# Ten patch chunks in f16 parts in place of eight, the normalised input written by ScalarE, its transposition behind four f16 chunks

## What is computed

```python
patches = X.reshape(B, C, 8, 28, 8, 28).transpose(0, 2, 4, 1, 3, 5).reshape(B, 64, 2352)
tokens = einsum('bpi,hi->bph', patches, W) + b          # 2352 -> 128
h = concatenate([cls, tokens], axis=1) * pos_embed      # 65 tokens of 128
h = h + lstm(layernorm(h))                              # 65 steps over the tokens
h = h + moe(layernorm(h))                               # 16 experts, the best 2, 128 -> 512 -> 128, exact gelu
```

## Time and profile before

| | before |
|---|---|
| median of three executions | 693.02 |
| the profiled execution's own time | 692.99 |
| its span (first to last instruction) | 691.2 |
| PE busy | 622.2 (90%) |
| PE's weight loads busy | 589.8 (85%) |
| VectorE busy | 569.0 (82%) |
| ScalarE busy | 489.4 (71%) |
| GpSimd busy | 414.4 (60%) |
| mean granted clock of PE | 0.96 |

### The profile page before, as it was taken

How to read it: one execution, slowest core, us unless ns; L and a number is a source line. 1 busy time by engine, 2 the same in 40 slices (tenths; PEclk the granted TensorE clock), 3 DMA queues, 4 the chain that set the end, 5 groups by cost and what they waited for, 6 DMA issues and landing times.

```text
span 691.2 us, 24716 instructions
## 1 busy us (share of the span) xinstructions
PE 622.2 (90%) x7952; PEld 589.8 (85%) x7952; DVE 569.0 (82%) x1839; ACT 489.4 (71%) x1335; POOL 414.4 (60%) x446
## 2 busy tenths in 40 slices
PE   4899999999999999999999779999999999999400
PEld 4899999999999999999989668799888899889300
DVE  3787888888888888888898868988888888888487
ACT  3587777666666667665555467788888888888465
POOL 0133333587776776677577666777777666666500
PEclk9999999999999999999999889999999999999855
DMA  8987787787888888878862233455543343332198
GB/s 315 371 276 271 266 282 248 251 267 268 269 272 264 270 270 261 268 244 259 251 218 91 74 90 92 126 160 168 147 122 108 105 108 105 110 113 74 32 374 340
DMA packets 72472, 141.68 MB, mean 205 GB/s; under 512 B 13142, under 2 KB 55714, under 8 KB 64414
## 3 DMA queue, kind: packets, MB, share of 16 engines
q1 hardware_dynamic: 62704, 121.69, 55.1%
q0 software_dynamic: 9280, 17.21, 7.1%
q10 hardware_dynamic: 366, 1.21, 0.5%
HBM read 116.35 MB, written 25.66 MB: 205 GB/s over the span
## 4 chain that ended last, share of the span: by engine, by line
PE 63%; DVE 7%; DMA 4%; issue 3%; POOL 2%; ACT 2%; POOLq 0%; SPq 0%; ACTq 0%; DVEq 0%
PE bank L1137 22%; PE bank L1292 14%; PE bank L1310 14%; PE bank L1183 4%; DMA patches<-back 3%; PE bank L1147 3%; PE bank L1266 2%; PE bank L1152 1%; PE bank L1238 1%; POOL sent L1093 1%; DVE patches L987 1%; ACT patches L646 1%; PE bank L1209 1%; PE bank L1162 1%; PE bank L1172 1%
## 5 line engine op out<-in xcount | busy, mean ns | idle before, releaser
L1115 POOL DMA_INDIRECT back<-patches x160 | 156.5, 978 | 64.9 <-issue 53.2
L1137 PE MATMUL bank<-ws,patches 128*128 128x128 f32 (+1 forms) x1408 | 173.2, 279 | 9.1 <-DMA patches<-in_x 9.1
L1093 POOL DMA_INDIRECT sent<-pay,slot_own x130 | 151.6, 1166 | 39.4 <-issue 36.1
L1137 PEld LDWEIGHTS bank<-ws,patches 128*128 128x128 f32 (+1 forms) x1408 | 164.1, 194 | 9.2 <-issue 7.5
L609 ACT ACTIVATE bank<-bank,b1s 128x256 f32<-128x256 f32 x320 | 130.7, 453 | 37.1 <-PE bank L1292 36.7
L553 ACT ACTIVATE gate<-bank,lbias 128x128 f32<-128x128 f32 x260 | 74.1, 367 | 82.2 <-PE bank L1152 82.2
L987 DVE TENSOR_TENSOR patches<-bank,patches 128x512 f16<-128x512 f32 x160 | 109.4, 684 | 26.3 <-ACT patches L618 21.6
L1310 PE MATMUL bank<-ex_hi,patches 128*128 x1280 | 112.5, 220 | 3.6 <-DVE patches L1003 2.9
L1292 PE MATMUL bank<-patches,ex_hi 128*128 128x256 f16 x640 | 111.2, 276 | 2.5 <-DVE patches L987 1.5
L1105 POOL TENSOR_TENSOR rstd<-veps,cst 128x2 f32<-128x2 f32 (+1 forms) x68 | 57.4, 844 | 87.8 <-DVE veps L734 86.4
L618 ACT ACTIVATE patches<-bank 128x512 f16<-128x512 f32 x160 | 97.6, 611 | 0.0
(11 more groups left out here) (139 smaller groups left out, 1406.6 us busy)
## 6 DMA issues: line engine op xcount, KB each, us to landing
patches<-in_x SPq DMA_DIRECT2D x62, 1152.0 KB
patches<-sent SPq DMA_DIRECT2D x80, 130.0 KB
patches<-back SPq DMA_DIRECT2D x13, 640.0 KB, 6.5
ex_raw<-in_we SPq DMA_DIRECT2D x64, 128.0 KB
patches<-in_b SPq DMA_DIRECT2D x80, 64.0 KB
posr<-in_pos SPq DMA_DIRECT2D x65, 64.0 KB
out_tower<-h SPq DMA_DIRECT2D x13, 320.0 KB, 5.3
back<-patches POOLq DMA_INDIRECT x160
```

The costliest lines, as they stand in the source:

```text
L1093: pool.indirect_dma_start(sent, bass.IndirectOffsetOnAxis(ap=slot_own[:, g % 4, choice, col:col + 1], axis=0), pay[:, t % NP, :], None, bo ...
L1115: pool.indirect_dma_start(back, bass.IndirectOffsetOnAxis(ap=dsti[j % NO][:, k:k + 1], axis=0), yo[j % NO][:, k, :], None, bounds_check=2 ...
L1137: last = pe.matmul(bank_of, l, w_, start=(c == KS and k == 0), stop=(c == KS - 1 and k == 2))
```

## The change

The number of f16 chunks KS goes from 8 to 10 (so nine f32 products of a patch, the rest's among them, in place of eleven), the number of raw expert buffers NE from 7 to 5. `xn` is written by ScalarE, between the tanh and the second half of the split, as `h0 * rstd + shift2`; so `shift2` gets a second column for the input, written by one VectorE instruction for both rows, and a second buffer per column. VectorE's `xn` instruction goes. On PE `transpose_x` stands behind four f16 chunks of the projection instead of ahead of all of them. The lines that load the gelu table after the last tanh stand now under a condition on t0 = n + 2 that is false for n = T - 1 = 64, so they are never issued. The diff:

```diff
--- before.py
+++ after.py
@@ -30,7 +30,8 @@
 KC = IN_D // P
 KREST = IN_D - KC * P
 KBIAS = 64
-KS = 8
+KS = 10
+KMID = 4
 E, FF = 16, 512
 FC = FF // P
 TOKENS = T * B
@@ -47,7 +48,7 @@
 PIECE = 256
 PIECES = E * 2 * FF // PIECE
 TWICE = 16
-NE = 7
+NE = 5
 UG = 8
 SIZES = [8] * 6 + [6, 4, 4, 3]
 EARLY_GROUPS = 6
@@ -131,7 +132,7 @@
         mv = sb("mv", [P, 2, 2])
         veps = sb("veps", [P, 2])
         rstd = sb("rstd", [P, 2])
-        shift2 = sb("shift2", [P, 2])
+        shift2 = sb("shift2", [P, 2, 2])
         xn = sb("xn", [P, 2, HID])
         xT_hi = sb("xT_hi", [HID, 2, B], F16)
         xT_lo = sb("xT_lo", [HID, 2, B], F16)
@@ -572,6 +573,13 @@
                 if 0 <= n <= T - 1:
                     through(act, c_done, n)
                     act.activation(tc[:, :], c2, ACT.Tanh, scale=0.5).then_inc(tc_done, 1)
+                t0 = n + 2
+                if 0 <= t0 <= T - 1:
+                    act.wait_ge(shift_done, normed(n))
+                    if t0 >= 2:
+                        through(act, xT_ps, t0 - 2)
+                    act.activation(xn[:, t0 % 2, :], h0[:, t0 % 4, :], ACT.Identity, bias=shift2[:, n % 2, 0:1],
+                                   scale=rstd[:, 0:1]).then_inc(xn_done, 1)
                     if n == T - 1:
                         act.activation(warm[:, :], cst[:, C_ONE:C_ONE + 1], ACT.Gelu)
                 if halved:
@@ -581,10 +589,10 @@
                 t = token_at(shifts, n)
                 if t >= 0:
 
-                    through(act, shift_done, t)
+                    act.wait_ge(shift_done, normed(t + 1))
                     if t >= NP:
                         rows_sent(act, t - NP)
-                    act.activation(pay[:, t % NP, 0:HID], h1[:, t, :], ACT.Identity, bias=shift2[:, t % 2:t % 2 + 1],
+                    act.activation(pay[:, t % NP, 0:HID], h1[:, t, :], ACT.Identity, bias=shift2[:, (t + 1) % 2, 1:2],
                                    scale=rstd[:, 1:2]).then_inc(yn_done, 1)
                 t = n + 2
                 if 0 <= t <= T - 1:
@@ -740,20 +748,16 @@
                     through(dve, cab_done, n)
                     dve.scalar_tensor_tensor(c2, cab[:, 0, :], 0.5, cab[:, 1, :], ALU.mult, ALU.add).then_inc(c_done, 1)
                     routing(n)
-                def shift_of(t):
-
-                    dve.wait_ge(rstd_done, normed(t + 1))
-                    dve.scalar_tensor_tensor(shift2[:, t % 2:t % 2 + 1], mv[:, 1, 0:1], -1.0, rstd[:, 1:2], ALU.mult,
+                def shift_of(n, both):
+
+                    dve.wait_ge(rstd_done, normed(n))
+                    if n >= 1 and both.start == 0:
+                        through(dve, xn_done, n)
+                    dve.scalar_tensor_tensor(shift2[:, n % 2, both], mv[:, both, 0], -1.0, rstd[:, both], ALU.mult,
                                              ALU.mult).then_inc(shift_done, 1)
 
-                if pre and post:
-                    shift_of(t1)
                 if pre:
-                    dve.wait_ge(rstd_done, normed(n))
-                    if t0 >= 2:
-                        through(dve, xT_ps, t0 - 2)
-                    dve.tensor_scalar(xn[:, t0 % 2, :], src0, mv[:, 0, 0:1], rstd[:, 0:1], ALU.subtract,
-                                      ALU.mult).then_inc(xn_done, 1)
+                    shift_of(n, both)
                 if 0 <= n <= T - 1:
 
                     through(dve, tc_done, n)
@@ -767,7 +771,7 @@
                                       ALU.subtract).then_inc(h_lo_done, 1)
                 t = token_at(shifts, n)
                 if t + 2 > T - 2:
-                    shift_of(t)
+                    shift_of(t + 1, slice(1, 2))
                 t = n + 4
                 if 1 <= t <= T - 1:
 
@@ -1100,6 +1104,8 @@
             def power(n, both):
 
                 pool.wait_ge(veps_done, normed(n))
+                if 0 <= n + 1 <= T - 1:
+                    through(pool, xn_done, n + 1)
                 if n - 1 >= 1:
                     through(pool, yn_done, n - 2)
                 pool.tensor_tensor(rstd[:, both], veps[:, both],
@@ -1218,10 +1224,11 @@
                     if t == 1:
                         pe.wait_ge(setup_act, 2)
                         pe.wait_ge(setup_dve, 2)
+                    pe.wait_ge(lo_done, t)
+                    project(t, 0, KMID)
                     if n >= 0:
                         transpose_x()
-                    pe.wait_ge(lo_done, t)
-                    project(t, 0, KS).then_inc(tok_done, 1)
+                    project(t, KMID, KS).then_inc(tok_done, 1)
                 if n < 0 or t > T - 1:
                     transpose_x()
                 t = token_at(logits_at, n)
```

## The result

The changed kernel is slower by a third of a per cent: median 695.56 us against 692.81, ratio 1.0036, interval 1.0025 to 1.0047. On another chip, later, it was 694.70 against 692.63, ratio 1.0034 (1.0023 to 1.0045). The forecast was 691.6; the time lies in its range, on the other side of no change.

The account below looks back on a forecast made before the run. PE was taken to bound ordinary steps, VectorE some of steps 54 to 60. Terms (a) -5.2, (b) +0.2, (c) +2.0, start +1.4, end +0.2 sum to -1.4: 691.6 us from a 693.02 median, range 687.3 to 697.3.

Parts of the forecast that it names:

- the ring: Chain from h1 through VectorE and ScalarE back to h1: +0.44, making 5.46 in ordinary steps, 0.14 under PE's 5.60.
- (a): 43 recurrent steps, 1 to 18, 20 to 41 and 47 to 49: -0.12 us each, -5.2 in all.
- the start: Before step 0, recurrent weights behind xn and half split, xlo longer: +1.4 us, bounds +0.5 and +2.2.
- PE's part: Two chunks change from f32 to f16: 0.12 us less a step, to 5.60; transposition 0.21 later.
- (b): Nine steps like 53, and step 19: margin 0.48, 0.56 wanted, ending near 5.73 to 5.80; +0.2 in all.
- (c): Steps 54 to 60: five without VectorE margin +2.2, two with idle time -0.2; +2.0 in all.
- The end and the table load: Step 62 +0.3, step 61 -0.1, together +0.2; moved gelu table load 0, bounds -0.2 and +1.0.
- The first: Rival: PE keeps the pace everywhere, (b) gains and (c) loses little; near 687.4; chance 0.22.
- The second: Rival: the ring takes the pace, shift to xlo costing 0.25 more than summed; +5.6, 698.6; chance 0.15.
- The third: Rival: fewer expert buffers or late table load cost +1 to +2, 692.6 to 693.6; within the forecast's 0.63.
- what I listed as proof against me: Ordinary steps over 5.65, xlo not waiting for the split, or PE idling at the input products for xT_lo.

Follow-up runs that it names:

- split_first_k4: Changed kernel with only the swap: the second half of the split ahead of xn on ScalarE in every step; median 795.10 us, ratio 0.9894, slow chip.
- split_first_warm: Changed kernel with the split's second half ahead of xn, transposition behind six f16 chunks, gelu load behind the last tanh; 687.99 us, ratio 0.9930.
- before_same: The kernel before, unchanged, run for its profile on a chip where it takes 793 to 803 us; ratio 0.9993.
- ks10_dve: Kernel before with KS = 10, NE = 5 and transposition behind four chunks, xn left on VectorE; ratios 0.9934, 0.9937, 0.9953.
- after_warm: Changed kernel with the gelu table load behind the last tanh again; ratio 1.0054.
- before_ne5: Kernel before with NE = 5 in place of 7 and nothing else; ratio 1.0006.
- start_split_3: Changed kernel with both halves of the split ahead of xn only before step 0; median 800.27 us on a slow chip.
- split_first: Changed kernel with the split's second half ahead of xn in every step and transposition behind six chunks; ratios 0.9848 and 0.9854 on slow chips.

## Why the prediction was wrong

It summed -5.2 + 0.2 + 2.0 + 1.4 + 0.2 = -1.4 and measured +2.8, 4.2 more. PE's price and the ring's price in one step were right. Two terms were mis-sized: (a), -5.2 summed and -2.6 measured, and the start, +1.4 summed and +2.85 measured. That the time still lies in the stated range is no merit of the sum.

- **PE's part: right.** Ordinary steps went from 5.72 to 5.61 (summed 5.60), the transposition came 0.23 later (summed 0.21).
- **The ring in an ordinary step: right**, 0.16 of margin against 0.14 summed.
- **(a), 43 steps at -0.12: the step that failed, 2.6 of the 4.2.** The forty of them in steps 1 to 41 gave -2.39 where -4.8 was summed, the three in 47 to 49 gave -0.19 for -0.36. (Steps 1 to 41 read -2.86 with step 19, -0.47, in which before's power had stood behind a store; I had put it under (b).) First, steps 17, 25, 33 and 41 are not "caught up": they last 5.86, +0.14 each. There the shift comes at 2.52, and an addition of the logits stands between `xT_lo` and `h0`, which costs the ring 0.20 and was left out of it:

```profile
126.04 0.15 DVE L756 SCALAR_TENSOR_TENSOR shift<-mv,rstd 128x2 f32<-128x2 f32 x1
...
127.37 1.49 DVE L780 TENSOR_TENSOR xlo<-patches,xhi 128x1280 f16<-128x1280 f32 x1 [0.39 <-ACT xhi L536]
128.78 0.28 DVE L702 TENSOR_TENSOR xT_lo<-bank,xT_hi 128x128 f16<-128x128 f32 x1
128.98 0.28 DVE L862 TENSOR_TENSOR lg<-bank,rbs 128x128 f32<-128x128 f32 x1
129.18 0.28 DVE L718 SCALAR_TENSOR_TENSOR h<-bank,posr 128x128 f32<-128x128 f32 x1
129.38 0.28 DVE L724 SCALAR_TENSOR_TENSOR h<-bank,h 128x128 f32<-128x128 f32 x1
```

  Counted: 2.52 + 1.33 + 1.41 + 0.20 + 0.20 + 0.20 = 5.86. With the swap alone (split_first_k4) they take 5.61. This is 1.1 us.

  Second, from step 20 on ordinary steps alternate 5.66 and 5.61. PE waits for `xT_lo` ahead of the transposition of the output row (L1178), one instruction before the input products where I looked for that wait. The weight loads in such a step:

```profile
185.95 0.14 PEld L1168 LDWEIGHTS bank<-cst,h 128*128 128x128 f32 x1
186.12 0.14 PEld L1178 LDWEIGHTS bank<-cst,pay 128*128 128x128 f32 x1
```

  0.17 apart where 0.11 is usual, and `xT_lo` ended at 186.05 (185.77 + 0.28). In nearly every step from 17 to 46 this load starts 0.07 to 0.08 after the end of `xT_lo`, and from the start of `xT_lo` to the second `h1` behind it, it is never under 6.22. So there is a second, longer ring: `h1`, shift, `xlo`, `xT_lo`, then through the whole of PE's step back to `h1`, two steps in one round: 2.25 + 1.40 + 1.41 + 6.22 = 11.28, and 5.61 + 5.67 = 11.28. PE does not make up the time that it waits for `xT_lo`; this wait the prediction put at nothing. This reading is by the timeline and the waits in the code; no kernel without that wait was tried. In split_first_warm, whose `xT_lo` is earlier by 0.46, the alternation is gone (six other steps between 19 and 36 take 5.70 to 5.82, for which I have no cause), and steps 17 to 41 are 0.75 shorter.

  The alternation is 0.4 us. The rest is spread: steps 16, 24, 32 and 40 gained 0.06 each, steps 2 and 11 were 5.79 and 5.74 in this profile, and the others ended at 5.61 for 5.60.
- **(b): the number by luck.** The ten steps gave +0.05 for +0.2, but it is nine at +0.52 together and step 19 at -0.47. The sum was wrong in itself too: a margin of 0.48 less 0.44 leaves 0.04, so by its own terms VectorE's ring is 5.68, under 5.72, and not 0.08 over. It does read 5.66 in step 53 (2.51 + 1.34 + 1.41 + 0.20 + 0.20), yet the step lasts 5.83, with idle time ahead of `h1`:

```profile
329.79 0.28 DVE L702 TENSOR_TENSOR xT_lo<-bank,xT_hi 128x128 f16<-128x128 f32 x1
...
330.19 0.28 DVE L724 SCALAR_TENSOR_TENSOR h<-bank,h 128x128 f32<-128x128 f32 x1
...
335.66 0.28 DVE L718 SCALAR_TENSOR_TENSOR h<-bank,posr 128x128 f32<-128x128 f32 x1
336.02 0.29 DVE L724 SCALAR_TENSOR_TENSOR h<-bank,h 128x128 f32<-128x128 f32 x1
```

  The ring through PE gives it: 336.02 - 329.79 = 6.23, and steps 52 and 53 together 2.58 + 1.34 + 1.41 + 6.23 = 11.56 (5.73 + 5.83).
- **(c): right in kind, one step too few.** Six of the seven steps have no margin, and they grew by 0.36 to 0.49, 0.43 on the average for the 0.44 summed; step 55 lost 0.08. Together +2.49 for +2.0. Step 54, shift to `xlo` 1.34:

```profile
339.11 0.15 DVE L756 SCALAR_TENSOR_TENSOR shift<-mv,rstd 128x2 f32<-128x2 f32 x1
340.45 1.49 DVE L780 TENSOR_TENSOR xlo<-patches,xhi 128x1280 f16<-128x1280 f32 x1 [0.39 <-ACT xhi L536]
```

- **The start, 1.45 of the 4.2.** +1.4 was summed, and +2.85 came, over the bound of 2.2. The delay of one step was summed right and taken once; steps -2 and -1 pay it in turn, each with the same row:

```profile
17.69 0.16 DVE L756 SCALAR_TENSOR_TENSOR shift<-mv,rstd 128x1 f32<-128x1 f32 x1 [0.69 <-POOL rstd L1111]
19.04 1.49 DVE L780 TENSOR_TENSOR xlo<-patches,xhi 128x1280 f16<-128x1280 f32 x1 [1.19 <-ACT xhi L536]
...
24.39 0.16 DVE L756 SCALAR_TENSOR_TENSOR shift<-mv,rstd 128x1 f32<-128x1 f32 x1 [0.67 <-POOL rstd L1111]
25.73 1.49 DVE L780 TENSOR_TENSOR xlo<-patches,xhi 128x1280 f16<-128x1280 f32 x1 [1.19 <-ACT xhi L536]
```

  From the first use of `rstd` to `xlo` it is 1.35 and 1.34 where it was 0.26, and `xlo` itself is 0.27 longer: 2.18 for the order and 0.54 for `xlo`. From the landing to the first `h1`, with no fall of the clock to 0.50 behind 22 us, it is 14.42 in before_same, 14.85 in the three profiles of ks10_dve and 17.03 in after_warm: 0.43 for the ten chunks and 2.18 for the order. Besides, the first loads landed later by 1.06 in this profile. Over all profiles the first `h0` starts at 14.91 to 15.34 with eight chunks (five profiles) and at 15.10 to 16.81 with ten (thirteen), 0.7 later on the average; why is open, nothing was tried on it. A fall of the clock in the kernel before hid 1.14 of the cost in the first pair, and one in the changed kernel added 0.33.
- **The end and the table load:** 0.0 against +0.2 in steps 61 to 63, and 0 as taken (after_warm: at most 0.4).
- **The rivals.** The first fell with steps 54 to 60. The second named the right loser, the ring, but its extra 0.25 did not come. The third was ruled out by before_ne5 and after_warm. Of what I listed as proof against me, both came in part: steps over 5.65, every second one by 0.01 to 0.02, and PE idle for `xT_lo`, one instruction ahead of where I named it.

## What to carry to other kernels

When work moves to an engine with idle time, ask where in that engine's order it goes. An instruction that must wait for a late value holds everything behind it, and here the work behind it was wanted by the engine that makes the value: a ring. Putting the work that is ready ahead of the wait took 5.2 us out with the same instructions (start_split_3 to split_first_k4); with two more chunks ahead of the transposition and the table load moved back as well, +0.3% became -0.7%. And count a delay in every step of a pipeline's start that pays it, and the ring in the steps with extra work too. Follow each ring through every engine that waits in it: a margin of 0.16 on VectorE did not save PE from waiting for VectorE.

## What the runs showed that I had not expected

On three other chips the kernel before takes 793 to 803 us in place of 693. In the experts' stage PE idles there ahead of products with nothing in the profile to wait for: in the window 450 to 550 of before_same,

```profile
L1292 PE MATMUL bank<-patches,ex_hi 128*128 128x256 f16 x184 | 36.3, 286 | 12.6 <-issue 9.4 <-DVE patches L987 2.5
```

and steps 50 to 53 of the first stage last 6.7 to 6.9 each against 5.7. split_first has 5.61 there on such a chip as well. That is a part of why its ratio is 0.985 on them and split_first_warm's 0.993 on the other; the cause of neither was found.
